# Decay matrix of a state-space layer: a VectorE scan over rows that transfers spread, in place of triangular sums on TensorE

## What is computed

```
S = S * dA_t[:, :, None, None] + jnp.einsum('bh,bn,bhp->bhpn', dt_t, B_t, x_t)
y_t = jnp.einsum('bhpn,bn->bhp', S, C_t)
```

## Time and profile before

| | us |
|---|---|
| median of 3 runs | 1773.66 (1773.55 to 1775.12) |
| span of the profiled execution | 1773.4 |
| state-space layer in it | 626.5 to about 1165 |
| TensorE busy | 1747.5, 99% |
| VectorE busy | 1331.7, 75% |
| ScalarE busy | 942.5, 53% |
| GpSimd busy | 823.5, 46% |

### The profile page before, as it was taken

How to read it: one execution, slowest core, us unless ns; L and a number is a source line. 1 busy time by engine, 2 the same in 40 slices (tenths; PEclk the granted TensorE clock), 3 DMA queues, 4 the chain that set the end, 5 groups by cost and what they waited for, 6 DMA issues and landing times. The chain is left out here.

```text
span 1773.4 us, 35811 instructions
## 1 busy us (share of the span) xinstructions
PE 1747.5 (99%) x13280; PEld 1288.9 (73%) x13280; DVE 1331.7 (75%) x2317; ACT 942.5 (53%) x1421; POOL 823.5 (46%) x565
## 2 busy tenths in 40 slices
PE   7999999999999999999999999999999999999999
PEld 4588888888888844544444444645888888888888
DVE  7978777887775758778777777757887787877655
ACT  7754747447474465435445536334547465474653
POOL 2766436244362426446456456725335263352533
PEclk9999999999999999999999999999999999999999
DMA  8032131111313031212112112112121311112100
GB/s 332 25 90 43 47 89 25 64 42 48 89 28 115 0 104 34 63 36 62 56 35 68 56 36 69 36 60 42 48 43 47 89 42 48 45 45 65 42 24 24
DMA packets 125197, 104.49 MB, mean 59 GB/s; under 512 B 104001, under 2 KB 104513, under 8 KB 119745
## 3 DMA queue, kind: packets, MB, share of 16 engines
q1 hardware_dynamic: 125120, 103.60, 19.1%
HBM read 49.59 MB, written 25.17 MB: 42 GB/s over the span
## 5 line engine op out<-in xcount | busy, mean ns | idle before, releaser
L504 POOL TENSOR_TENSOR f_hlo<-f_h,f_hhi 128x768 f16<-128x768 f32 x135 | 201.9, 1495 | 600.0 <-ACT f_hhi L687 571.1
L1261 PE MATMUL f_gate_ps<-spare 128*128 128x256 f16 x2688 | 329.9, 272 | 0.2
L1185 PE MATMUL f_down_ps<-wd,f_hhi 128*128 128x256 fp8e4 x1440 | 318.4, 273 | 0.7 <-DVE xa L882 0.7
L1185 PE MATMUL f_down_ps<-wd,f_hlo 128*128 128x256 fp8e4 x1440 | 318.4, 273 | 0.0
L1261 PEld LDWEIGHTS f_gate_ps<-spare 128*128 128x128 fp8e4 x2688 | 254.8, 97 | 45.2 <-issue 2.0
L1261 PE MATMUL f_up_ps<-spare,wu 128*128 128x256 f16 x1792 | 229.9, 273 | 0.1
L1261 PEld LDWEIGHTS f_up_ps<-spare,wu 128*128 128x128 fp8e4 x1792 | 172.8, 98 | 23.3 <-issue 0.7
L882 DVE SCALAR_TENSOR_TENSOR xa<-f_down_ps,out_scale,xa 128x512 f32<-128x512 f32 x195 | 136.4, 743 | 59.2 <-PE f_down_ps L1185 58.9
L1648 POOL TENSOR_TENSOR s_am<-s_tri,s_al 128x512 f16<-128x512 f16 x128 | 151.1, 1210 | 18.8 <-DVE s_al L1920 18.8
L1185 PEld LDWEIGHTS f_down_ps<-wd,f_hhi 128*128 128x128 f16 x1440 | 140.8, 98 | 17.8 <-issue 1.6
L1185 PEld LDWEIGHTS f_down_ps<-wd,f_hlo 128*128 128x128 f16 x1440 | 140.9, 98 | 16.3
(11 more groups left out here) (247 smaller groups left out, 3294.9 us busy)
## 6 DMA issues: line engine op xcount, KB each, us to landing
xa<-res SPq DMA_DIRECT2D x16, 1024.0 KB, 5.4
res<-xa SPq DMA_DIRECT2D x15, 1024.0 KB, 3.9
res<-xa SPq DMA_DIRECT2D x34, 256.0 KB, 2.0
xa<-in_u SPq DMA_DIRECT2D x8, 1024.0 KB, 4.8
xa<-res SPq DMA_DIRECT2D x32, 256.0 KB, 2.7
late<-in_w_gate SPq DMA_DIRECT2D x4, 1024.0 KB, 17.1
spare<-in_w_up SPq DMA_DIRECT2D x3, 1024.0 KB, 8.9
late<-in_w_in SPq DMA_DIRECT2D x1, 2320.0 KB, 8.3
```

The lines of the kernel that those rows point to most:

```text
L504: last = nc.gpsimd.tensor_tensor(hlo[:, p, a:b, :], src, hhi[:, p, a:b, :], ALU.subtract)
L1185: last = nc.tensor.matmul(at, part[:, p, kind, m * P:(m + 1) * P], wd[:, weight, p, :], start=(p == 0 and part is hhi and (m == 0 or name ...
L1261: last = nc.tensor.matmul(acc[:, j * HT:(j + 1) * HT], w[:, k, e * P:(e + 1) * P], xop[part][:, o, k, :, :], start=(fresh and (j, k, part) ...
```

## The change

The sums are replaced by running products.

- `turn_decays` turns the group's 128 x 32 tile of a(t) into 32 rows (chunk, head) by 128 tokens. ScalarE takes the exponential twice, into `zrow` (first column kept at 0) and `arow`. VectorE scans `arow` into `erow` (a running product, `begin_decays`), so a row is E.
- `keep_rows` writes both sets of rows to memory. `spread_z` reads one chunk's row of 1024 values into all 128 partitions (512 KB), `spread_e` each half of E's row into 64 partitions (256 KB together). Both are double-buffered.
- `scan`: one VectorE instruction per chunk, 128 x 1024, state = state * z + eye, where `eye` (float16) has a one at i = j in each head. The zero at each head's start ends the head before it. The result `lt` is L, its last columns the decays to the end.
- `inner`: one GpSimd instruction of 128 x 1024 multiplies L by B·C, which ScalarE (`copy_bt`) copies from its bank with B. GpSimd's `masked`, VectorE's `gm`, `btok` and masking, ScalarE's two exponentials, TensorE's `chunk_decays` and `sum_decays` go.
- `chunk_start`, `inner`, `readout` (cd) and `direct` (dx) now run one chunk ahead. `turn_x` stands first in a chunk, ahead of `transposes(front, 2, 4)` in the first.
- The normalization moves from VectorE (`normalize`) to ScalarE (`normal`), with a small added VectorE and GpSimd instruction for its bias.
- `softplus_end` for `LAST` moves from chunk 3 of `EVE` to its chunks 1 and 2; it loses two small steps everywhere.
- y gets two banks, the state and B·C a bank each. `dx`, `dtxe`, `yv`, `bt`, `db`, `lt` lie in tiles that were free in this layer.

```diff
-al = sb(ctx, "s_al", [P, B, 2, CH, H], F16)
...
-dec = sb(ctx, "s_dec", [P, B, CH * H + CH * H // 2])
-am = sb(ctx, "s_am", [P, 2, H, P], F16)
-lx = sb(ctx, "s_lx", [P, H, P])
-ecb = sb(ctx, "s_ecb", [P, H // 2, P])
+zrow = sb(ctx, "s_zrow", [P, P])
+arow = sb(ctx, "s_arow", [P, P])
+erow = sb(ctx, "s_erow", [P, P])
+zeros = sb(ctx, "s_zeros", [P, P])
+z_rows = nc.dram_tensor("s_z_rows", (B, CH, H * P), F32, kind="Internal").ap()
+e_rows = nc.dram_tensor("s_e_rows", (B, CH, H * P), F32, kind="Internal").ap()
+db = spare[:, 5120:7168].rearrange("p (s n) -> p s n", s=2)
+lt = spare[:, 7680:9728].rearrange("p (s n) -> p s n", s=2)
+eb = sb(ctx, "s_eb", [P, 2, H // 2, P])
+lx = sb(ctx, "s_lx", [P, 2, H, P])
+eye = sb(ctx, "s_eye", [P, H * P], F16)
 cd = sb(ctx, "s_cd", [P, H // 2, P])
-btok = parts[7]
-gm = parts[8]
+bt = parts[9].rearrange("p (s n) -> p s n", s=2)
 dtx = sb(ctx, "s_dtx", [P, D])
...
+dx, dtxe = xa[:, 1, 0, :].rearrange("p (k i) -> p k i", k=KD), xa[:, 1, 1, :]
+yv = parts[8].rearrange("p (k i) -> p k i", k=KD)
...
-seg = ps(ctx, "s_seg", [P, H * P])
+y_all = ps(ctx, "s_y", [P, 2 * D])
+y_ps = y_all[:, :].rearrange("p (r x) -> p r x", r=2)[:, :, 0:D // 2]
...
+        def spread_z(f, c):
...
+            sp.wait_ge(z_out, 16 * (order(f) + 1))
+            sp.sem_inc(sp_free, 1)
+            if f is not FIRST:
+                sp.wait_ge(scan_done, after(CH * order(f) + c - 1))
+                sp.sem_inc(sp_free, 1)
+            sp.dma_start(db[:, c % 2, :], z_rows[f[1], c:c + 1, :].to_broadcast([P, H * P])).then_inc(db_in[c % 2], 16)
...
+        def spread_e(f, c):
...
+            sp.wait_ge(e_out, 16 * (order(f) + 1))
+            sp.sem_inc(sp_free, 1)
+            if f is not FIRST:
+                sp.wait_ge(s1_done, after(CH * order(f) + c - 1))
+                sp.sem_inc(sp_free, 1)
+            for r in range(2):
+                sp.dma_start(eb[half(r), c % 2, :, :].rearrange("p h i -> p (h i)"),
+                             e_rows[f[1], c:c + 1, r * H * P // 2:(r + 1) * H * P // 2].to_broadcast([N, H * P // 2]))\
+                  .then_inc(eb_in[c % 2], 16)
...
+        def keep_rows(f):
+            sp.wait_ge(z_done, after(order(f) + 1))
+            sp.sem_inc(sp_free, 1)
+            sp.dma_start(z_rows[f[1], :, :].rearrange("c (h i) -> (c h) i", h=H), zrow[0:CH * H, :]).then_inc(z_out, 16)
+            sp.wait_ge(e_done, after(order(f) + 1))
+            sp.sem_inc(sp_free, 1)
+            sp.dma_start(e_rows[f[1], :, :].rearrange("c (h i) -> (c h) i", h=H), erow[0:CH * H, :]).then_inc(e_out, 16)
...
+            for c in range(CH):
+                if c < CH - 1:
+                    spread_e(g, c + 1)
+                if c < CH - 2:
+                    spread_z(g, c + 2)
...
-        def masked(g, c):
...
-            for part in range(2):
-                for r in range(2):
-                    last = nc.gpsimd.tensor_tensor(
-                        am[:, part, 4 * r:4 * r + 4, :],
-                        tri16[:, :].unsqueeze(1).to_broadcast([P, H // 2, P]),
-                        al[:, g[1], part, c, 4 * r:4 * r + 4].unsqueeze(2).to_broadcast([P, H // 2, P]),
-                        ALU.mult)
-                last.then_inc((am_high_done, am_done)[part], 1)
...
+        def inner(g, c):
...
+            pool.wait_ge(scan_done, after(q + 1))
+            pool.wait_ge(bt_done, after(q + 1))
+            if g is not FIRST:
+                pool.wait_ge(y_done, after(q - 1))
+            nc.gpsimd.tensor_tensor(lx[:, c % 2, :, :], lt[:, c % 2, :].rearrange("p (h i) -> p h i", h=H),
+                                    bt[:, c % 2, 0:P].unsqueeze(1).to_broadcast([P, H, P]), ALU.mult)\
+              .then_inc(lx_done, 1)
...
-            nc.scalar.activation(dec[:, f[1], :], src[:, 0:CH * H + CH * H // 2], ACT.Exp, scale=1.0 / AS)\
-              .then_inc(free, 1)
+            nc.scalar.activation(zrow[0:CH * H, 1:P], src[0:CH * H, 1:P], ACT.Exp).then_inc(z_done, 1)
+            nc.scalar.activation(arow[0:CH * H, :], src[0:CH * H, 0:P], ACT.Exp).then_inc(free, 1)
+        def copy_bt(g, c):
...
+            q = CH * order(g) + c
+            act.wait_ge(bc_done, after(q + 1))
+            if g is not FIRST:
+                act.wait_ge(st_done, after(q - 1))
+            nc.scalar.activation(bt[:, c % 2, :], bc[:, 0:P + N], ACT.Copy).then_inc(bt_done, 1)
...
+        def normal(f):
...
+            act.wait_ge(nmr_done, after(order(f)))
+            act.wait_ge(tr_done, after(KD * order(f)))
+            for c in range(CH):
+                last = nc.scalar.activation(xn[:, c, :], xa[:, 2, c, :], ACT.Identity,
+                                            bias=nmr[:, c:c + 1], scale=rstd[:, c:c + 1])
+            last.then_inc(xn_done, 1)
...
-                nc.scalar.activation(lx[:, :, :].rearrange("p h i -> p (h i)"), seg[:, :], ACT.Exp,
-                                     scale=1.0 / AS).then_inc(lx_done, 1)
-                act.wait_ge(cb_done, after(q + 1))
-                act.wait_ge(cd_done, after(q))
-                nc.scalar.activation(ecb[:, :, :].rearrange("p h i -> p (h i)"), turn[:, :], ACT.Exp,
-                                     scale=1.0 / AS).then_inc(ecb_done, 1)
+                if (n := next_chunk(g, c, front)) is not None:
...
+        def begin_decays(f):
...
+            nc.vector.tensor_tensor_scan(erow[0:CH * H, :], arow[0:CH * H, :], zeros[0:CH * H, :], 1.0,
+                                         ALU.mult, ALU.add).then_inc(e_done, 1)
+        def scan(g, c):
...
+            q = CH * order(g) + c
+            dve.wait_ge(db_in[c % 2], 16 * loaded(g, c))
+            if g is not FIRST:
+                dve.wait_ge(dtxe_done, after(q - 1))
+                dve.wait_ge(lx_done, after(q - 1))
+            nc.vector.tensor_tensor_scan(lt[:, c % 2, :], db[:, c % 2, :], eye[:, :], 0.0,
+                                         ALU.mult, ALU.add).then_inc(scan_done, 1)
...
-                nc.vector.tensor_tensor(gm[:, :], bc[:, 0:P], tri[:, :], ALU.mult).then_inc(gm_done, 1)
-                dve.wait_ge(st_done, after(q))
-                nc.vector.tensor_copy(btok[:, :], bc[:, P:P + N]).then_inc(btok_done, 1)
-                dve.wait_ge(lx_done, after(q + 1))
-                dve.wait_ge(gm_done, after(q + 1))
-                nc.vector.tensor_tensor(lx[:, :, :], lx[:, :, :],
-                                        gm[:, :].unsqueeze(1).to_broadcast([P, H, P]), ALU.mult)\
-                  .then_inc(m_done, 1)
...
+                if c < CH - 1:
+                    scan(g, c + 1)
...
+                    if c == CH - 1:
+                        scan(front, 0)
...
-        def chunk_decays(g, c, between=None):
...
-            for part in range(2):
-                if part:
-                    pe.wait_ge(am_done, after(q + 1))
-                    pe.sem_inc(pe_free, 1)
-                for r in range(2):
-                    last = nc.tensor.matmul(turn[half(r), :], ones16[:, 0:N],
-                                            am[:, part, 4 * r:4 * r + 4, :].rearrange("p h i -> p (h i)"),
-                                            start=(part == 0), stop=(part == 1), skip_group_check=True)
-            last.then_inc(cb_done, 1)
-            if between is not None:
-                transposes(between, 2, 4)
-            pe.wait_ge(lx_done, after(q))
-            for r in range(2):
-                for part in range(2):
-                    last = nc.tensor.matmul(seg[:, r * 512:(r + 1) * 512], after16[:, :],
-                                            am[:, part, 4 * r:4 * r + 4, :].rearrange("p h i -> p (h i)"),
-                                            start=(part == 0), stop=(part == 1))
-            last.then_inc(seg_done, 1)
+            nc.tensor.matmul(acc[0:CH * H, 0:P], a32, ident[:, :], start=True, stop=True).then_inc(dec_in, 1)
...
                     transposes(front, 0, 2)
-                    chunk_decays(g, c, front)
+                    turn_x(g, c)
+                    transposes(front, 2, KD)
                 else:
-                    chunk_decays(g, c)
-                chunk_start(g, c)
+                    turn_x(g, c)
+                if (n := next_chunk(g, c, front)) is not None:
+                    chunk_start(*n)
                 if c:
                     project_out(g, c - 1)
                 elif g is LAST:```

The order on the engines, word for word as the two programs have them. TensorE, chunk 2 of a group in the loop, from the state product of chunk 1 on (`s_turn<-s_am` and `s_seg` are the sums, `s_turn<-ident` is x turned, L2059 a block of the convolution, L2167 and L2174 y, L2095 the gate). Before:

```order
L2187 MATMUL s_mix<-s_dtxe,late 64x256 x2
L2119 REGISTER_ALU
L2127 MATMUL s_turn<-s_am,late 64x512 x4
L2136 MATMUL s_seg<-s_am,s_after 128x512 x4
L2148 MATMUL s_mix<-spare,s_xc 128x128
L2149 MATMUL s_mix<-ident,s_xc 128x128
L2197 MATMUL s_out<-late,s_yv 128x512 x4
L2155 MATMUL s_turn<-ident,s_xc 128x128 x4
```

305 lines of the change are left out of this document (144 added, 161 removed).

## The result

The changed kernel takes 1742.51 us (median of 4 runs, 1741.59 to 1743.55) against 1773.61 (1773.34 to 1775.12): ratio 0.9822, interval 0.9808 to 0.9836. Forecast was 1744, range 1726 to 1767. The profiled execution has a span of 1741.8 us against 1773.4, so 31.6 are to be found in the traces. Where both are on record the time is some 1.7 us above the span (1743.55 and 1741.8 for this one), so the span of 1773.4 must belong to the execution of 1775.12, the longest of its four (the others took 1773.34 to 1773.66); the profile after is the longest of its four as well.

The account below looks back on a forecast made before the run. The prediction took TensorE, busy 99% of the span, to bound the kernel. Its terms, 51 - 8.4 - 3.2 - 8 - 1.5 - 1 = 29 us, taken from 1773.4 gave 1744, range 1726 to 1767.

Parts of the forecast that it names:

- TensorE's 51 us: Over the whole layer: removed sums, 45.1 us in 32 chunks, with turned columns and waits, take 51 us off TensorE.
- (a): Chunks 1 and 2: `dtx` late and VectorE held by GpSimd's `inner`, 1.4 us a group in six groups, 8.4.
- (b): Start of a group: only B·C now follows the transposes, so TensorE waits 0.45 us in seven groups, 3.2.
- (c): EVE's start to LAST's first y: VectorE's longer round gives back 8 of the 9.5 us freed.
- (d): LAST: the scan fits without convolution; 0.5 us in three chunks where `yv` stands behind `inner`, 1.5.
- (e): Opening: ScalarE's first normalizations delay TensorE's banks and first rows must return from memory, 1 us (0 to 3).
- The scan: VectorE's 128 x 1024 instruction per chunk: 2.2 us taken, between bounds of 1.2 and 6.3.
- Rival 1: Scan at full rate, 1.2 us; all of (a) and 3 of EVE's 8 vanish: 1733; chance 0.17.
- The trip: Rows through memory, a 512 KB spread taking 3.6 us: covered by 2 to 4 us at the next group's first scan.
- Rival 2: VectorE instructions wait out GpSimd's, with `inner` at 3.6 to 4.1 us: 19 us more, 1763; chance 0.19.
- Rival 3: A scan of 6.3 us makes VectorE the bound: 1809; decides from a scan of 3.9 us; chance 0.09.
- Rival 4: Rows' trip some 8 us longer, each of eight groups waits 3.6 us, no gain: 1773; chance 0.05.

Follow-up runs that it names:

- run 1: Changed kernel with eight float16 products of the removed sums' shapes put back on TensorE as dead work in each chunk: 1774.9 us.
- run 2: Changed kernel with the scan replaced by a plain product of the same two tiles, leaving the running product out: 1735.7 us.
- run 7: Changed kernel with the product with B·C moved from GpSimd back to VectorE, right behind the scan: 1761.5 us.
- run 3: Changed kernel with every 128 x 1024 scan issued twice, the second after the first, same result: 1807.5 us.
- run 10: Changed kernel with the spread of each group's first row sent twice, the second after the first has landed: 1751.6 us.
- Runs 4 to 6: Changed kernel with VectorE reordered: `dtx` ahead of the scan, 1740.9; `yv` ahead of the state product, 1744.5; both, plus a LAST scan moved later, 1736.9 us.

## Why the prediction was right, point by point

**TensorE's 51 us** came out as about 44.5. The 1.41 us a chunk was the length of the eight products; taken out they give 1.25 (run 1), since the state product and x turned each run 0.05 to 0.1 longer next to each other than next to float16 products: 0.16 x 32 = 5. The turned columns take 0.34, not 0.12, so that term gave nothing instead of 1.4. Lesson of this step: the difference of two starts is right only while the neighbours stay the same.

**(a) VectorE late in chunks 1 and 2, 8.4 us:** the step that failed. In the loop it was 0: run 2 shows the same 62.37 us with a cheap instruction. `dtx` arrived 0.2 us ahead of y. I had it 0.8 late and went up to 1.4 for `inner`, which took 2.0 and not 2.5. Of the 1.0 between 0.8 late and 0.2 early, 0.15 is TensorE's chunk, which shrank by 1.25 and not 1.4; most of the rest is a term that I had put at nothing. The work of VectorE from y to the scan takes 8.71 us (811.51 to 820.22) where up to the first replaced instruction it took 9.39 (821.01 to 830.40), because the lighter GpSimd holds it up less (each of its long rows stands beside a GpSimd instruction). The three convolution steps at its end, before and after:

```profile
827.27 3.21 DVE L1863 SCALAR_TENSOR_TENSOR s_xc<-s_xpad,late,s_xc 128x512 f32<-128x512 f32 x3
```

```profile
817.98 2.32 DVE L1926 SCALAR_TENSOR_TENSOR s_xc<-s_xpad,late,s_xc 128x512 f32<-128x512 f32 x3
```

They, `yv` and a softplus step together are 2.5 us shorter, the state product, a statistics step and the added bias step some 1.8 longer. So the scan's added 0.7 was paid by 0.7 less of being held up. Waits of this kind came only in the first group, 0.43 and 0.23 for `dtx` and 1.47 for `yv`, and there VectorE had just waited 1.03 and 2.02 us for rows from memory, so part of them belongs to the trip. Mechanism right, margin mis-sized: run 7, with 1.2 us more ahead of `dtx`, makes a loop group 63.8, and run 3, with 2.3 more, about 70.

**(b) The start of a group, 0.45 x 7:** 0.40 x 7, as forecast.

**(c) EVE, 8 of 9.5 given back:** the stretch gained 1.9, and 0.4 went to `xnt`, so about 7.2 of 9.5. Only part of it is the round that was forecast: y of chunk 2 comes 13.42 us after y of chunk 1 (1071.24 and 1057.82), of which 3.04 is waiting, so 13.4 and 10.4 where 11.5 to 14 and 10 were forecast. With the 0.30 of chunk 1 that is 3.3 us. The lower clock behind it, 1.6, and the 2.53 for `inner` behind a second scan at LAST's start were not in the prediction; that the sum came near 8 is luck. **(d) LAST:** 1.1 worse than forecast: 0.81 for `yv` and 0.23 for `dtx`, as the kind was forecast, and 1.7 of lower clock behind the 2.53, which was not. **(e) The opening:** 0.4 of 1.

**The scan:** 2284 ns against 2.2 forecast. The Trainium skill, "DVE: opcode table, instruction layouts, handler registers and perf-mode slots", section 6, has the built-in scan at half throughput. The trace agrees: 2284 ns is 1.9 times the 1218 of run 2's plain product of the same tiles. Rival 1 (full rate) falls. Run 2 gives its price, 1735.7; the 1733 worked out is near it by luck, since 8.4 of its 11 us were to come out of (a), most of it in the loop, where run 2 gained nothing.

**The trip:** forecast covered by 2 to 4 us; the cover in the loop is at least 4.0 (run 10). What I had not seen is that lateness on SyncE's queue hurts first through the load behind it.

**Rival 2 (shared way):** the mechanism is in the trace (`yv` at 1528 behind `dx` or `cd`, `inner` at 3.90 once), but with `inner` at 2.0 its cost shows only at the ends. Runs 4 to 6 show how the order on VectorE decides there. **Rival 3:** run 3 leaves its decision point possible (between 2.3 and 4.6 us), its price was too low. **Rival 4:** the gain is there; run 1 shows that it is TensorE's time. Its sum was wrong too: cover, TensorE's 7 us and a wait of 3.6 are 13 to 15 us more, not 8, which makes it less likely than it was given.

So the total, 31.1 us by the medians and 29.7 in the profiles without the feed-forward behind, against 29, was close by luck, because two errors met: some 6.5 us less taken out of TensorE, 7.5 less given back (about 14.5 for 22). The profiles have 1.8 us more from the feed-forward behind, which can't be put down to the change.

## What to carry to other kernels

Here, with one engine busy 99%, work taken off it shortened the time one for one wherever no input of it came late. So write down, per chunk, by how many tenths of a microsecond each input is early, and count what gets shorter on the engine that takes the work over as well as what gets longer: the term left out here was as large as the one counted. A wait can pass from one input to the next when one is made earlier: two moves gave nothing alone, and with a third 5.6 us together. The stretches at the ends, where the pipeline has less other work, gave back most of what was lost here, so they are worth ordering apart. A transfer with slack of its own may still hold a queue on which a transfer without slack stands.
